# The second absorbed attention: probabilities times folded values as three float16 products

## The reference, cut to what matters

```python
def _L2_xattn_ref(hidden_q, kv_c, Wq, w_kc_q, w_kc_kv, W_qr, W_kr, Wo):
    ...
    q_hk = (hidden_q @ Wq.T).reshape(b, s, H, K)            # 16 heads of 128
    q_big = jnp.einsum('bshk,hkq->bshq', q_hk, w_kc_q)
    kv_rope = kv_c * cos[None] + _rotate_half(kv_c) * sin[None]
    q_r = jnp.einsum('bshq,hqr->bhsr', q_big, W_qr)
    k_r = jnp.einsum('bld,hdr->bhlr', kv_rope, W_kr)
    scores = jnp.einsum('bhsr,bhlr->bhsl', q_r, k_r)
    attn = jax.nn.softmax(scores, axis=-1)
    ctx_c = jnp.einsum('bhsl,bld->bhsd', attn, kv_rope)
    ctx_lat = jnp.einsum('bhsd,hkd->bshk', ctx_c, w_kc_kv)
    out = ctx_lat.reshape(b, s, H * K) @ Wo.T
    return out

x = x + _L2_xattn_ref(_layernorm(x, axis=-1), ctx_512, L2_xattn_Wq, ...)
```

## Time and profile before

| | |
|---|---|
| median of 3 runs | 1296.74 us (1294.53 to 1297.24) |
| the profiled execution | 1295.07 us, its span 1293.2 us |
| busy, of the span | PE 1203.8 us (93%), DVE 882.1 (68%), ACT 508.9 (39%), POOL 376.6 (29%) |
| mean granted clock of TensorE | 0.979 of full speed |
| chain that ended last | PE 76%, DVE 15%, issue 3%, ACT 3% |
| the fold | about 623.5 to 664.1 us of the span |
| the halves | about 664.1 to 726.8 us |

### The profile page before, as it was taken

How to read it: one execution, slowest core, us unless ns; L and a number is a source line. 1 busy time by engine, 2 the same in 40 slices (tenths; PEclk the granted TensorE clock), 3 DMA queues, 4 the chain that set the end, 5 groups by cost and what they waited for, 6 DMA issues and landing times.

```text
span 1293.2 us, 21914 instructions
## 1 busy us (share of the span) xinstructions
PE 1203.8 (93%) x8483; PEld 783.6 (61%) x8483; DVE 882.1 (68%) x1713; ACT 508.9 (39%) x1141; POOL 376.6 (29%) x393
## 2 busy tenths in 40 slices
PE   6889999999799999999999889999999888999997
PEld 4664559999545565566657546664565565465565
DVE  3777966767476766667667697877666666766666
ACT  3423360111233433343443236643433343555553
POOL 1540216556203333334113310001333342233332
PEclk9889999999899999999999999999999989999999
DMA  4030140000143444444320000001443200233442
GB/s 144 2 155 21 56 165 6 2 1 2 64 159 115 123 124 124 116 115 117 133 84 1 17 1 1 2 1 39 135 115 118 83 17 2 88 114 115 122 127 82
DMA packets 41544, 97.19 MB, mean 75 GB/s; under 512 B 5446, under 2 KB 18246, under 8 KB 39392
## 3 DMA queue, kind: packets, MB, share of 16 engines
q1 hardware_dynamic: 41440, 95.79, 24.0%
HBM read 94.35 MB, written 1.42 MB: 74 GB/s over the span
## 4 chain that ended last, share of the span: by engine, by line
PE 76%; DVE 15%; issue 3%; ACT 3%; POOL 1%; DMA 1%; SPq 0%; DVEq 0%; POOLq 0%; ACTq 0%
PE PS L1401 10%; PE PS L1402 10%; PE PS L1403 10%; PE PS L1446 4%; PE PS L1448 4%; PE PS L1447 4%; PE PS L1036 3%; PE PS L1054 2%; PE PS L1220 2%; PE PS L2103 2%; PE PS L1022 2%; PE PS L1024 2%; PE PS L1023 2%; PE PS L2120 2%; DVE small L547 1%
## 5 line engine op out<-in xcount | busy, mean ns | idle before, releaser
L1618 POOL TENSOR_TENSOR arena<-arena,m_g 128x512 f32<-128x512 f32 x142 | 182.3, 1285 | 413.9 <-DMA m_g<-gate_rows 246.3
L1401 PE MATMUL PS<-arena 128*128 128x512 f16 x608 | 232.2, 382 | 3.6 <-DVE arena L1553 2.0
L1402 PE MATMUL PS<-arena 128*128 128x512 f16 x608 | 232.1, 382 | 0.0
L1403 PE MATMUL PS<-arena 128*128 128x512 f16 x608 | 232.0, 382 | 0.0
L1446 PE MATMUL PS<-arena 128*128 128x256 f16 x608 | 165.8, 273 | 11.0 <-DVE arena L1573 8.3
L1448 PE MATMUL PS<-arena 128*128 128x256 f16 x608 | 165.7, 273 | 0.0
L1447 PE MATMUL PS<-arena 128*128 128x256 f16 x608 | 165.7, 273 | 0.0
L1513 ACT ACTIVATE arena<-PS 128x512 f32<-128x512 f32 x112 | 66.9, 597 | 247.8 <-PE PS L1403 237.4
L1556 DVE SCALAR_TENSOR_TENSOR arena<-arena,PS 128x512 f32<-128x512 f32 x112 | 76.9, 687 | 117.1 <-ACT arena L1513 116.8
L1573 DVE TENSOR_TENSOR arena<-arena 128x512 f16<-128x512 f32 x142 | 110.1, 775 | 3.7 <-ACT arena L1523 3.7
L1403 PEld LDWEIGHTS PS<-arena 128*128 128x128 f16 x608 | 59.9, 98 | 72.8 <-issue 2.0
(11 more groups left out here) (282 smaller groups left out, 2284.5 us busy)
## 6 DMA issues: line engine op xcount, KB each, us to landing
w_stage<-in_up SPq DMA_DIRECT2D x80, 256.0 KB, 2.8
m_g<-gate_rows SPq DMA_DIRECT2D x70, 256.0 KB, 4.2
arena<-in_heads SPq DMA_DIRECT2D x16, 1088.0 KB, 5.1
w_stage<-in_down SPq DMA_DIRECT2D x80, 128.0 KB, 4.1
m_g<-gate_rows SPq DMA_DIRECT2D x17, 512.0 KB, 4.0
m_g<-gate_rows SPq DMA_DIRECT2D x6, 448.0 KB, 4.1
m_g<-gate_rows SPq DMA_DIRECT2D x6, 384.0 KB, 4.3
m_g<-gate_rows SPq DMA_DIRECT2D x6, 320.0 KB, 4.2
```

Source lines behind the costliest of these rows:

```text
L1401: pe.matmul(to, w_hi, x_hi, start=(k == 0), stop=False)
L1402: pe.matmul(to, w_lo, x_hi, start=False, stop=False)
L1403: ins = pe.matmul(to, w_hi, x_lo, start=False, stop=(k == KT - 1))
L1618: pool.tensor_tensor(m_c[:, st % 2, :], m_b[:, st % LAG, :], m_g[:, st // 2 % 2, st % 2, :], ALU.mult).then_inc(s.c, 1)
```

## The change

Folded values and transposed probabilities are kept as two float16 parts each, both scaled by 64, and each float32 product of the output becomes three float16 products (high x high, high x low, low x high). x is summed with the factor 1/4096.

- ScalarE writes the high parts of both (the same instructions as before, now into float16).
- VectorE writes the low parts: in the fold two instructions for each pair (`dve_values_low`), behind the low parts of the keys; in the halves one for each event (`low(n - 2)` in iteration n), behind `summed(n)`. A new semaphore, `turned`, counts the latter. `output(n)` and `transposed(n)` wait for it where they waited for ScalarE's.
- `s.f`, which `values(q)` waits for at 2q, is now counted once by ScalarE and once by VectorE for each pair.
- VectorE's loop over the halves is put into another order: iteration n is `softened(n + 1)`, `summed(n)`, `low(n - 2)`, `added`, where it was `softened(n)`, `summed(n)`, `added`.
- Two small semaphores of other stages (`rr`) are merged into others of the same stage; the same waits stay.

```diff
-        plain_pt = [take(a, [1024])[0] for a in (10240, 18432)]
+        plain_pt = [take(a, [2, 1024], F16)[0] for a in (10240, 18432)]
...
+        plain_f = at_f.bitcast(F16).rearrange("p (a b j c) -> p a b j c", a=2, b=B, j=PAIRS)
...
             def values(q, c):
                 act.wait_ge(s.f_ps, q + 1)
-                act.activation(fold_f[:, c::2, q, :], PS[:, (5, 7)[c], :].rearrange("p (b c) -> p b c", b=2),
-                               ACT.Copy).then_inc(s.f, 1)
+                ins = act.activation(plain_f[:, 0, c::2, q, :], PS[:, (5, 7)[c], :].rearrange("p (b c) -> p b c", b=2),
+                                     ACT.Copy, scale=SPLIT)
+                if c:
+                    ins.then_inc(s.f, 1)
...
+        def dve_values_low(q):
+
+            dve, s = nc.vector, att[2]
+            dve.wait_ge(s.f, 2 * q + 1)
+            for c in range(2):
+                hi, lo = (plain_f[:, a, c::2, q, :] for a in range(2))
+                ins = dve.scalar_tensor_tensor(lo, PS[:, (5, 7)[c], :].rearrange("p (b c) -> p b c", b=2), SPLIT, hi, ALU.mult, ALU.subtract)
+            ins.then_inc(s.f, 1)
...
                 dve_keys_low(q - 1)
+                dve_values_low(q - 1)
...
             def transposed(n):
                 if n >= 2:
-                    pe.wait_ge(soft.t, PLAIN_0 + n - 1)
+                    pe.wait_ge(s.turned, n - 1)
...
             def output(n):
                 b, half, q = plain_event(n)
-                pe.wait_ge(soft.t, PLAIN_0 + n + 1)
+                pe.wait_ge(s.turned, n + 1)
...
                 for j in range(4 * half, 4 * half + 4):
-                    ins = pe.matmul(PS[:, (5, 7)[q], 0:D], plain_pt[q][:, j * P:(j + 1) * P], fold_f[:, b, j, :],
-                                    start=(j == 0), stop=(j == PAIRS - 1))
+                    to, (p_hi, p_lo) = PS[:, (5, 7)[q], 0:D], (plain_pt[q][:, a, j * P:(j + 1) * P] for a in range(2))
+                    f_hi, f_lo = (plain_f[:, a, b, j, :] for a in range(2))
+                    pe.matmul(to, p_hi, f_hi, start=(j == 0), stop=False)
+                    pe.matmul(to, p_hi, f_lo, start=False, stop=False)
+                    ins = pe.matmul(to, p_lo, f_hi, start=False, stop=(j == PAIRS - 1))
...
             def added(b, q):
-                dve.tensor_tensor(tile, tile, PS[:, (5, 7)[q], 0:D], ALU.add).then_inc(soft.x, 1)
+                dve.scalar_tensor_tensor(tile, PS[:, (5, 7)[q], 0:D], UNSPLIT, tile, ALU.mult, ALU.add).then_inc(soft.x, 1)
...
+            def low(n):
+                b, half, q = plain_event(n)
+                hi, lo = (plain_pt[q][:, a, half * 512:(half + 1) * 512] for a in range(2))
+                dve.wait_ge(soft.t, PLAIN_0 + n + 1)
+                dve.scalar_tensor_tensor(lo, PS[:, n % 2, :], SPLIT, hi, ALU.mult, ALU.subtract).then_inc(s.turned, 1)

             softened(0)
             dve_keys_low(PAIRS - 1)
-            summed(0)
-            for n in range(1, 4 * B + 4):
+            dve_values_low(PAIRS - 1)
+            for n in range(4 * B + 4):
+                if n + 1 < 4 * B:
+                    softened(n + 1)
                 if n < 4 * B:
-                    softened(n)
                     summed(n)
+                if 2 <= n < 4 * B + 2:
+                    low(n - 2)
                 if n >= 6 and n % 4 >= 2:
                     added((n - 6) // 4, n % 2)
```

More of the change, by code:

```diff
@@ L209, in build @@
         att = {1: Sems("att1", "w0 w1 zero a_ps a al eb_ps eb m_ps m f_ps f xl tab q_ps roped r s"),
-               2: Sems("att2", "w0 w1 bt_ps bt e_ps e m_ps mh m f_ps f c_ps c dt_ps dt q s")}
-        pre = [Sems("pre0", "w fold_ps fold ms r z zT_ps zT biased y_ps ssq rr z2 z2T_ps h low"),
+               2: Sems("att2", "w0 w1 bt_ps bt e_ps e m_ps mh m f_ps f c_ps c dt_ps dt q s turned")}
+        pre = [Sems("pre0", "w fold_ps fold ms r z zT_ps zT biased y_ps ssq z2 z2T_ps h low"),
                Sems("pre1", "w h low logit e t"),
                Sems("pre2", "w hT z zT_ps ms r qkv biased copied qr qrT_ps qhi qT s mx p pt_ps pt one oneT_ps oneT v pv o y_ps x2 "
-                    "ssq rr z2 z2T_ps h low logit e t"),
+                    "ssq z2 z2T_ps h low logit e t"),
                Sems("pre3", "w h low logit lg t")]
@@ L1247, in evacuated @@
                     act.wait_ge(soft.y_ps, 2 * NT + QT * (b - 1) + q + 1)
-                act.activation(plain_pt[q][:, half * 512:(half + 1) * 512], PS[:, n % 2, :], ACT.Copy).then_inc(soft.t, 1)
+                act.activation(plain_pt[q][:, 0, half * 512:(half + 1) * 512], PS[:, n % 2, :], ACT.Copy, scale=SPLIT).then_inc(soft.t, 1)
             act_keys_high(PAIRS - 1)
@@ L1760, in pool_pre0 @@
                 pool.tensor_tensor(p0_h[:, i, :], xn[:, i, :], p0_bias, ALU.add).then_inc(s.biased, 1)
-            pool_pow(pre[0].ssq, 1, rms_r[:], rms_e[:], pre[0].rr)
+            pool_pow(pre[0].ssq, 1, rms_r[:], rms_e[:], pre[0].r)
             nc.gpsimd.wait_ge(pre[0].low, NT // 2)
@@ L1809, in dve_pre0 @@
             dve.tensor_scalar(rms_e[:], p0_ssq, 1.0 / D, RMS_EPS, ALU.mult, ALU.add).then_inc(s.ssq, 1)
-            dve.wait_ge(s.rr, 1)
+            dve.wait_ge(s.r, 2)
             for i in range(NT):
@@ L2279, in pool_pre2 @@
             pool_values(me)
-            pool_pow(pre[2].ssq, 1, rms_r[:], rms_e[:], pre[2].rr)
+            pool_pow(pre[2].ssq, 1, rms_r[:], rms_e[:], pre[2].r)
         def dve_pre2():
```

## The result

The changed kernel takes 1376.35 us (median of 4 runs, 1374.11 to 1379.75) where the kernel before takes 1296.09 on the same chip (4 runs, 1294.53 to 1297.24): a ratio of 1.061 with an interval of 1.059 to 1.063, some 80 us slower. The forecast was 1374. The profiled execution took 1379.75 us, its span 1377.9.

What follows compares the result with a forecast made beforehand. TensorE was taken to bound both attention stages without a hole. Fold 21, halves 31 and clock 27 us sum to 79, so 1295.07 + 79 = 1374 us, range 1343 to 1393.

Steps and rivals of the forecast that it cites:

- What bounds: Attention, fold and halves: TensorE is the bound with no hole, so whatever makes it wait is paid in full.
- The fold: Fold: `values(q)` waits for VectorE's values' low parts, 2.96 us in each of seven pairs, the first longer; +21 us.
- The halves: Halves: VectorE's iteration and TensorE's output and scores run in turn, 5.81 us an event against 3.46; +31 us.
- The skew as the larger part: Halves: VectorE's order by one half is the larger part; with the old order about 7 us for 16 events.
- The clock: Fold and halves: the holes make TensorE's granted clock fall; +27 us, with 0 and 50 as its ends.
- The clock full: Rival for the attention: both loops close but the clock stays full; 1295 + 52 = 1347 us, chance 0.18.
- Clock low throughout: Rival for the attention: clock at its lower level throughout; 1295 + 52 + 50 = 1397 us, chance 0.05.
- The faster rival: Halves: VectorE waits for nothing, 3.16 us an event, 4.8 us less; 1290 us; chance 0.03 for faster or unchanged.
- 155 to 185 us: Profile sign: the attention from `folded(0)` to the last sum takes this long instead of 103 us.
- the lower price: New VectorE instructions, fold and halves: 0.60 us each if they fit the step alone, 2 us off the total.
- The loop of the halves alone: Rival: only the loop in the halves closes; 1295 + 47 = 1342 us, chance 0.07 for one loop only.
- that of the fold: Rival: only the fold's loop closes, with its clock; 1295 + 32 = 1327 us, chance 0.07 for one loop only.

Runs made afterwards that it cites:

- e2: Changed kernel with the values' low parts at the head of VectorE's fold iteration, ahead of the copy that waits for `chained`: 1345.45 us, 1.035 of the kernel before.
- e1: Changed kernel with VectorE's loop over the halves back in the order of before, `softened(n)` then `summed(n)`: 1340.68 us, 1.031 of the kernel before.
- e3: Changed kernel with VectorE's old order in the halves and the values' low parts at the head of the fold iteration: 1305.20 us, 1.004 of the kernel before.
- e6: Changed kernel with 216 useless products filling TensorE's idle places ahead of `values` and the outputs, all waits kept: 1346.14 us, 1.036 of the kernel before.
- e4: Changed kernel with values' low parts early and TensorE issuing `scores(n + 1)` ahead of the output, VectorE's skew kept: 1295.81 us, 0.997 of the kernel before.
- e8: Kernel before with VectorE's skewed order in the halves and `added` at the head of its iteration: 1299.45 us, 1.001 of the kernel before.
- e9: Changed kernel with values' low parts early, and `low` and `added` at the head of VectorE's iteration; TensorE's order untouched: 1304.06 us, 1.004 of the kernel before.
- e5: Kernel before with only VectorE's skewed order in the halves, float32 products, no low parts: 1312.28 us, 1.010 of the kernel before.
- e10: e4 with the first pair's values' low parts between the second and third of VectorE's eight token normalisations: 1291.68 us, 0.994 of the kernel before.
- e7: Kernel before with VectorE's skewed order and `scores(n + 1)` ahead of the output on TensorE, float32 products: 1296.04 us, 0.998 of the kernel before.

## Why the prediction was right, point by point

**What bounds.** TensorE had no hole and every stall came out in full: 83.8 of 84.7 us lie in the two stages, nothing was hidden.

**The fold, 21 us.** Right. Seven stalls, 20.7 us in the waits (forecast 7 x 2.96, the first 0.7 longer: 6 x 2.87 and 3.46 measured), and 20.5 in the run with the clock at full. The order was the reason, not the two instructions: with the same two moved (e2), 29.4 of the fold's 36.0 us go.

**The halves, 31 us.** Right in mechanism and nearly in size: 29.3 us at full clock. The closed loop is 5.68 us for an event where I had added up 5.81; the difference lies in `low`, which took 0.64 us for my 0.69, and in the time from its end to the start of the output, 789.38 - 789.32 = 0.06 us for the 0.14 of the earlier trace rows. The values' low parts took 0.68. Of the count, 13 outputs wait for VectorE where I had 12 loops, 5 of them for the sum into x where I had 6.

**The skew as the larger part.** Right: of the 47.8 us in the halves 8.4 are left in e1, and 5.8 in e3 at full clock, forecast 7.

**The clock, 27 us.** This is the term that was too small: 34 us by stage lengths, 33 by the ratios. In the fold it was 15.5 for 11, in the halves 18.5 for 15.6. I had let a fall in the fold cost half of "3 to 5 us" of the following stretch, once in each pair. The rows show it lasting longer: behind three of the seven stalls `values` takes 1.98 or 1.99 us, all of it at the lower level (1.09 at the full one), behind two 1.22 and 1.31, and at the first pair of e2, with no further hole, the clock stayed down for nearly 10 us. Windows of the changed fold:

```profile
640.00:645.00 5.00, 4.94 (x24) 4.10 (x23) 0.25 (x2) 1.47 (x3) 0.00 (x0) 0.50 0.58 214
645.00:650.00 5.00, 2.19 (x18) 1.16 (x20) 2.66 (x5) 0.15 (x1) 0.00 (x0) 0.50 0.00 0
650.00:655.00 5.00, 5.00 (x36) 3.37 (x34) 1.60 (x4) 2.69 (x6) 0.00 (x0) 0.80 0.64 221
655.00:660.00 5.00, 2.13 (x22) 1.16 (x23) 2.68 (x5) 0.88 (x3) 0.00 (x0) 0.88 0.01 2
660.00:665.00 5.00, 5.00 (x36) 3.37 (x32) 1.60 (x4) 2.37 (x6) 0.00 (x0) 0.78 0.69 242
```

In the halves I had half of 12 events at 2.6 us. Of the 12 events from 713.15 to 799.54 two take 5.67 and 5.68 us and the other ten 7.04 to 8.59, so falls came in nearly all and held for a part of each.

The Trainium skill's page "TensorE: Matmul & The Clock Gate", section "Why this matters for your kernels", would have kept the clock full over holes of this length, but for the longest, the 3.46 us of the first pair. The trace does not agree: in the window from 655 to 660, with the hole of 2.87 us that ends at 658.07, the clock falls to a mean of 0.88, and in the next, where TensorE is busy all 5 us, it is 0.78; with the holes filled it is 1.00 throughout. Its "A second HAM failure mode: psum-queue depth-cycling", by which short pauses make the clock swing, agrees with these windows.

**The sum.** 21 + 31 + 27 = 79 was forecast; 20.5 + 29.3 + 34 = 83.8 is what the profiles show. The profiled execution of after is the slowest of its four, 3.4 us above their median; by medians the change costs 80.3 us. So the closeness to the forecast is in part luck: the clock's 7 us too few are made up for by that, and by 0.13 us too many in each event.

**The rivals.** The clock full: e6 shows what that would have given: 47 us over the kernel before by the medians and 49.8 by stage lengths, forecast 52. That its median, 1346.14, is so near the forecast of 1347 is chance, since the kernel before takes 1299.53 on that chip. Clock low throughout: no, 0.75 and 0.81. The faster rival named the point from which it would decide, scores of the next event ahead of the output that waits for `low`. e4 puts them there: 1295.81 on a chip where the kernel before takes 1300.31, 4.5 us less, forecast 4.8; the halves are 4.6 shorter in its profile and the fold 1.9 longer. Its events with `added` are 3.5 us, as forecast, those without 2.7 to 3.04, the mean 3.17, forecast 3.16.

**One forecast of the profile was off.** The attention was to take 155 to 185 us; it takes 187.2, the clock again.

**Slips in the sums that change nothing.** With the low parts in, VectorE has about 8 of the fold's 39 us free and not 14: 39 - 21.83 = 17.2, less 14 x 0.61 = 8.5; the changed fold keeps it busy 8.4 us longer (32.31 against 23.90). The sum for the clock full and the lower price is 1295 + 52 - 2 = 1345, while the range begins at 1343, and its end at 1393 has no working. The loop of the halves alone (1342) lies outside the range as well as that of the fold.

## What to carry to other kernels

Before an engine gets a new instruction that another engine waits for, write down what stands ahead of it in its own row and what each of those waits for: if one of them waits for work that the waiting engine has queued behind the wait, the two engines run in turn, and the price is the whole row per turn and not the new instruction. A loop skewed on one engine has to be skewed on the engine that feeds it too (e4), or everything that the feeding engine waits for has to be moved ahead of the skewed step (e8, e9); here moving two steps, the low parts on VectorE and the scores on TensorE, turned 80 us lost into a small gain. And count the clock with such stalls: it took 34 us on top of 50.

## What the runs showed of the hardware

- A hole of 1.42 us (the first pair in e2, e3 and e9) was each time followed by nearly 10 us at the 1.2 GHz level, though TensorE was busy all of it: in e2 busy 9.42 of 9.42 us, clock 0.56. I had expected 3 to 5 us. The hole isn't the only thing that can do it: the layer ahead leaves TensorE busy 3.3 to 4.3 of 5 us for some 15 us or more, and behind that e4, e5 and e10 show a shorter fall near the first pair without this hole (fold 1.6 to 1.9 us longer), while before, e7 and e8 show none.
- Useless products in the holes are worth their place when the holes can't be closed: 33 us gained in e6.
- Twelve float16 products of 256 columns took 790.70 - 789.38 = 1.32 us in the changed kernel, the forecast 1.31 from a feed-forward layer; at the lower level one starts 0.21 us behind the other instead of 0.11 (717.16 and 717.37, the same kernel).
- From the end of a VectorE instruction to the TensorE instruction that waits for it the timelines show 0.06 us (`low` to the output, 789.32 to 789.38) to 0.15 us (the sum into x in e5, 693.19 to 693.34).
- Of two candidates that end 0.04 us apart a trace can name the wrong one as the releaser: at the outputs of e5 it names ScalarE, and e8, which moves VectorE's sum into x alone, takes the wait away.
